# Cross-attention with a routed block: queries and keys in matmuls of 512 columns for four batches, GpSimd's instructions in an alternating order, and another order of the first slots

## The reference

```python
b, tq, _ = input.shape                      # 128, 128, 256
q = (input @ Wq + bq).reshape(b, tq, H, D).transpose(0, 2, 1, 3)
kv = (encoded_features @ Wkv + bkv).reshape(b, tk, 2, H, D).transpose(2, 0, 3, 1, 4)
scores = jnp.einsum('bhqd,bhkd->bhqk', q, kv[0]) / math.sqrt(D)
attn = jax.nn.softmax(scores, axis=2)
out = jnp.einsum('bhqk,bhkd->bhqd', attn, kv[1])
out = out.transpose(0, 2, 1, 3).reshape(b, tq, H * D) @ Wo + bo
...
scores = jnp.einsum('bld,d->bl', x, w_router)           # routed block
_, top_idx = jax.lax.top_k(scores, int(L * 0.75))       # 96 of 128 tokens
processed = jax.nn.gelu(jnp.einsum('bkd,de->bke', selected, w_block))
out = x.at[batch_idx, top_idx].set(processed)
...
x = x + attention(layernorm(x), ctx_1024)
x = x + routed_block(layernorm(x))
```

## Time and profile before

| | us |
|---|---|
| median of 3 runs | 902.03 (901.85 to 904.2) |
| the profiled execution, its device time | 903.28 |
| its span, first to last instruction | 901.5 |
| PE busy in the span | 868.3 (96%) |
| PE weight load | 755.4 (84%) |
| DVE | 854.4 (95%) |
| ACT | 872.5 (97%) |
| POOL | 795.0 (88%) |

### The profile page before, as it was taken

How to read it: one execution, slowest core, us unless ns; L and a number is a source line. 1 busy time by engine, 2 the same in 40 slices (tenths; PEclk the granted TensorE clock), 3 DMA queues, 4 the chain that set the end, 5 groups by cost and what they waited for, 6 DMA issues and landing times. The chain is left out here.

```text
span 901.5 us, 31626 instructions
## 1 busy us (share of the span) xinstructions
PE 868.3 (96%) x10562; PEld 755.4 (84%) x10562; DVE 854.4 (95%) x2068; ACT 872.5 (97%) x4632; POOL 795.0 (88%) x1487
## 2 busy tenths in 40 slices
PE   7899999999999999999999999999999999999972
PEld 6688888888888888888888888888888888888852
DVE  6889999999999999999999999999999999999987
ACT  5899999999999999999999999999999999999984
POOL 4568889999999999999999999999999999998865
PEclk9999999999999999999999999999999999999996
DMA  6221223233233223223223233223222222312102
GB/s 202 61 68 51 65 67 93 59 87 93 59 88 96 59 86 95 59 87 94 69 78 92 60 89 91 76 71 91 79 73 88 82 70 86 96 43 55 49 25 93
DMA packets 70978, 70.48 MB, mean 78 GB/s; under 512 B 12064, under 2 KB 62752, under 8 KB 70816
## 3 DMA queue, kind: packets, MB, share of 16 engines
q1 hardware_dynamic: 69456, 67.68, 26.2%
q10 hardware_dynamic: 1360, 0.79, 0.3%
HBM read 35.13 MB, written 16.78 MB: 58 GB/s over the span
## 5 line engine op out<-in xcount | busy, mean ns | idle before, releaser
L593 ACT ACTIVATE e_sb<-ps_s,neg_max 128x128 f32<-128x128 f32 x2048 | 770.0, 607 | 3.6 <-DVE neg_max L751 3.3
L593 ACT ACTIVATION_READ_ACCUMULATOR e_sb<-ps_s,neg_max 128x1 f32 x2048 | 704.0, 431 | 0.0
L751 DVE TENSOR_REDUCE neg_max<-ps_s 128x4 f32<-128x512 f32 x512 | 331.8, 668 | 25.8 <-PE ps_s L349 24.4
L349 PE MATMUL ps_s<-q_eo,k_sb 32*128 32x256 f32 x2048 | 146.6, 400 | 2.3 <-DVE recip L804 1.4
L414 PE MATMUL ps_a<-e_sb,v_pad 128*32 128x128 f32 x4096 | 138.4, 276 | 2.1 <-POOL v_pad L1085 0.9
L310 PE MATMUL ps_a<-w_o_sb,o_sb 128*128 128x256 f32 x512 | 133.2, 383 | 3.2 <-DVE v_sb L858 3.0
L414 PEld LDWEIGHTS ps_a<-e_sb,v_pad 128*32 128x32 f32 x4096 | 104.1, 109 | 23.7 <-issue 21.3
L349 PEld LDWEIGHTS ps_s<-q_eo,k_sb 32*128 32x128 f32 x2048 | 94.0, 184 | 30.8 <-issue 26.0
L1085 POOL TENSOR_TENSOR v_pad<-v_sb,recip 128x256 f32<-128x256 f32 x128 | 79.7, 623 | 31.8 <-DVE recip L811 29.8
L1074 POOL TENSOR_TENSOR x_sb<-x_sb,bo_sb 128x256 f32<-128x256 f32 x128 | 106.2, 831 | 0.2
L303 PE MATMUL ps_t<-w_z_hi,xt_hi 128*128 128x258 f32 x256 | 96.4, 376 | 2.2 <-DVE z_sb L870 2.2
(11 more groups left out here) (109 smaller groups left out, 2465.5 us busy)
## 6 DMA issues: line engine op xcount, KB each, us to landing
x_sb<-in_x SPq DMA_DIRECT2D x64, 256.0 KB, 2.9
c_sb<-in_ctx SPq DMA_DIRECT2D x64, 256.0 KB, 3.1
out<-z_sb SPq DMA_DIRECT2D x64, 256.0 KB, 2.4
q_eo<-q_raw SPq DMA_DIRECT2D x504, 32.0 KB, 2.0
z_sb<-in_L_xattn_Wkv ACTq DMA_DIRECT2D x2, 256.0 KB, 7.4
z_sb<-in_L_xattn_Wq ACTq DMA_DIRECT2D x1, 256.0 KB, 4.2
w_z_sb<-in_L_ffn_w_block SPq DMA_DIRECT2D x1, 256.0 KB, 7.7
w_o_sb<-in_L_xattn_Wo SPq DMA_DIRECT2D x1, 256.0 KB, 7.0
```

Source lines behind the costliest of these rows:

```text
L349: mm = nc.tensor.matmul(ps_s[:, bank(b, j), c, :, :], k_sb[rows, r2, c, h * T:(h + 1) * T], q_eo[rows, r2, :, c, h, :], start=True, stop=True)
L593: last = nc.scalar.activation(e_sb[:, b % 4, j, c, par, :], ps_s[:, bank(b, j), c, par, :], ACT.Exp, bias=neg_max[:, b % 4, h:h + 1], accu ...
L751: nc.vector.tensor_reduce(neg_max[:, b % 4, :].rearrange("p (c j q) -> p j c q", c=C, j=J)[:, j, :, :], ps_s[:, bank(b, j), :, :, :], AX.X ...
```

## The change

1. *Queries and keys.* From batch 8 on they are made for four batches at once. In step s the new `queries_or_keys(s)` makes one half of the features (m) of queries (s mod 4 = 0, 1) or keys (2, 3) of batches 4(s div 4) + 4 to + 7, in six matmuls of 512 columns. DVE's `queries(b, m)` and `keys(b, m)` add the bias as a column of scalars (tensor_scalar). The first eight batches keep pairs (`..._of_pair`). SP copies each half as it comes, eight DMAs in each of two steps.
2. *Distance and rings.* Inputs are transposed eight batches ahead (LEAD = 8) instead of five; steps 2 and 3 take two batches each. `t_hi` and `t_lo` hold three groups of four batches, `e_sb` three batches, x 18.
3. *POOL's order* in a step: instructions with one tensor and scalars take turns with those of two tensors. The variance and the root of `rstd1` and `rstd2` are parted, with `values_over_sums` between them; `gelu_product` comes a step later.
4. *First slots.* `queries(2)` before `weights_low("v")`; `scores(1)` and its exps before the block weights' mean and the inputs of batch 5; more context loads ahead of the first query DMAs on SP.
5. *The router's keep row* is transposed from 128 rows, the others zero, with three more memsets or parts of memsets at the start of POOL.

```diff
+    RX = 18
+    LEAD = 8
+    FIRST_QUAD = 8
...
-        t_hi = sb("t_hi", [P, 4, 2, C, 2 * T], f32r)
+        t_hi = sb("t_hi", [P, 3, 2, C, 4 * T], f32r)
...
-        e_sb = sb("e_sb", [P, 4, J, C, 2, T])
+        e_sb = sb("e_sb", [P, 3, J, C, 2, T])
...
+            def queries_even_odd(b, m):
+
+                if has(b) and b >= FIRST_QUAD:
+                    n = (b // 4) % 2
+                    sp.wait_ge(q_raw_ready, b + 2 + 2 * m)
+                    if m == 0:
+                        sp.wait_ge(s_mm[J - 1], b - 4)
                     for par in range(2):
                         for j in range(J):
                             rows = slice(32 * j + D * par, 32 * j + D * par + D)
-                            sp.dma_start(q_eo[rows, n, par, :, :, :], q_raw[rows, n, :, :, :]).then_inc(q_eo_in[n], 16)
+                            sp.dma_start(q_eo[rows, n, par, m, :, :], q_raw[rows, m, :]).then_inc(q_eo_in[n], 16)
...
+            for s in range(3, B + 18):
+                if s % 4 == 0:
+                    queries_even_odd(s + 4, 0)
+                elif s % 4 == 1:
+                    queries_even_odd(s + 3, 1)
+                if s >= 4:
+                    load_c(s + 12)
                 store(s - 17)
-                load_x(s + 13)
+                load_x(s + 15)
...
+            def queries_or_keys(s):
+
+                b, kind, m = s // 4 * 4 + 4, s % 4 // 2, s % 2
+                if not has(b):
+                    return
+                w = "qk"[kind]
+                pe.wait_ge(xt_ready, upto(s - 4))
+                if kind == 0 and m == 0:
+                    pe.wait_ge(t_lo_ready, upto(b + 3))
+                mm = three_terms(ps_q[:, :],
+                                 lambda a, c: (w_hi, w_lo)[a][w][:, c, m * P:(m + 1) * P],
+                                 lambda a, c: (t_hi, t_lo)[a][:, (b // 4) % 3, kind, c, :])
                 mm.then_inc((q_mm, k_mm)[kind], 2)
...
             scores(0)
-            queries_or_keys(2, 0)
+            queries_or_keys_of_pair(2, 0)
             transpose_inputs(4)
-            queries_or_keys(2, 1)
+            queries_or_keys_of_pair(2, 1)
+            scores(1)
             mean_of_block_weights()
             transpose_inputs(5)
-            scores(1)
             values(0)
             transpose_inputs(6)
-            queries_or_keys(4, 0)
-            pair_ready(2)
+            queries_or_keys_of_pair(4, 0)
+            transpose_inputs(7)
+            queries_and_keys_ready(2)
             attention(0)
 
             for s in range(2, B - 1):
                 sure = 20 <= s < B - 8
                 scores(s)
-                transpose_inputs(s + 5, s > 2)
+                if s < 4:
+                    transpose_inputs(2 * s + 4)
+                else:
+                    transpose_inputs(s + LEAD, s > 4)
                 values(s - 1)
-                queries_or_keys(s + 2, 1, sure)
-                queries_or_keys(s + 3, 0, sure)
+                if s < 4:
+                    queries_or_keys_of_pair(2 * s, 1)
+                else:
+                    queries_or_keys(s)
                 keep_columns(s - 16)
                 candidates(s - 12)
                 projection(s - 2, sure)
-                pair_ready(s + 1, sure)
-                inputs_ready(s + 6)
+                queries_and_keys_ready(s + 1)
+                if s < 4:
+                    transpose_inputs(2 * s + 5)
+                if s == 2:
+                    queries_or_keys_of_pair(6, 0)
+                if s >= 4:
+                    inputs_ready(s + LEAD + 1)
                 block_product(s - 4, sure)
...
             exps(0, 1)
             exps(0, 0)
+            exps(1, 3)
             inputs_high(5)
-            exps(1, 3)
             exps(1, 2)
             inputs_high(6)
             exps(1, 1)
+            inputs_high(7)
...
-                inputs_high(s + 5, sure)
+                inputs_high(s + LEAD if s >= 4 else 2 * s + 4)
                 exps(s, 3, sure)
                 exps(s, 2)
+                if s < 4:
+                    inputs_high(2 * s + 5)
                 exps(s, 1)
...
+            def queries(b, m):
+
+                if has(b):
+                    dve.wait_ge(q_mm, b + 2 + 2 * m)
+                    if b == FIRST_QUAD:
+                        dve.wait_ge(q_eo_pair_in[4], 128)
+                        dve.wait_ge(q_eo_pair_in[6], 128)
+                    else:
+                        dve.wait_ge(q_eo_in[(b // 4 - 1) % 2], stripes(b - 4))
+                    nc.vector.tensor_scalar(q_raw[:, m, :], ps_q[:, :], bq_sb[:, m:m + 1], None,
                                             ALU.add).then_inc(q_raw_ready, 2)
...
             for j in (3, 2, 1, 0):
                 maxima(0, j)
+            queries_of_pair(2)
             weights_low("v")
-            queries(2)
             inputs_low(4)
+            inverse_sums_23(0)
+            keys_of_pair(2)
             stats1_of_pair(6)
-            keys(2)
-            centre_block_weights()
-            inverse_sums_23(0)
             maxima(1, 3)
             maxima(1, 2)
+            centre_block_weights()
+            inverse_sums_01(0)
+            maxima(1, 1)
             inputs_low(5)
-            inverse_sums_01(0)
             values_and_bias(0)
-            maxima(1, 1)
             maxima(1, 0)
             inputs_low(6)
+            inverse_sums_23(1)
             stats1_of_pair(8)
-            queries(4)
-            inverse_sums_23(1)
+            queries_of_pair(4)
+            inputs_low(7)
+            stats1_of_pair(10)
...
-                normalise(s + 7, sure)
-                rstd1_of_pair(s + 9)
-                rstd2_of_pair(s - 4)
-                gelu_square(s - 5, sure)
+                normalise(s + LEAD + 1, sure)
+                gelu_square(s - 5)
+                variance1_of_pair(s + 11)
+                variance2_of_pair(s - 4)
                 values_over_sums(s - 1, sure)
+                root1_of_pair(s + 11)
+                root2_of_pair(s - 4)
                 scale_and_shift(s - 16)
                 unprocessed(s - 16, sure)
+                input_and_bias(s + 2)
                 gelu_factor(s - 5)
+                gelu_product(s - 8)
                 gelu_sum(s - 7)
-                input_and_bias(s + 4)
                 gelu_cubic(s - 5)
-                gelu_product(s - 7)
```

More of the change, by code:

```diff
@@ L152, in landed, with pair_x, landed_x @@
             return b // R * 16 + 16
-        x_in = [sem(f"x_in{i}") for i in range(8)]
+        def pair_x(b):
+            return b % RX // 2
+        def landed_x(b):
+            return b // RX * 16 + 16
+        x_in = [sem(f"x_in{i}") for i in range(RX // 2)]
         c_in = [sem(f"c_in{i}") for i in range(8)]
@@ L245, in store, with queries_even_odd_of_pair @@
                                  z_sb[:, b % R:b % R + 2, 0:E]).then_inc(stored[pair(b)], 16)
-            def queries_even_odd(b):
-                if b % 2 == 0 and b >= 2 and has(b):
-                    n = (b // 2) % 2
-                    if b == 2:
-                        sp.wait_ge(q_eo_zero, 1)
-                    sp.wait_ge(q_raw_ready, upto(b + 1))
-                    if has(b - 4):
-                        sp.wait_ge(s_mm[J - 1], upto(b - 3))
+            def queries_even_odd_of_pair(b):
+                if b == 2:
+                    sp.wait_ge(q_eo_zero, 1)
+                if b == 4:
+                    sp.wait_ge(q_eo_zero, 2)
+                sp.wait_ge(q_raw_ready, b + 2)
+                n, h = (b // 4) % 2, b % 4
+                for par in range(2):
+                    for j in range(J):
+                        rows = slice(32 * j + D * par, 32 * j + D * par + D)
+                        sp.dma_start(q_eo[rows, n, par, :, h:h + 2, :],
+                                     q_raw[rows, :, h * T:(h + 2) * T]).then_inc(q_eo_pair_in[b], 16)
+            def queries_even_odd(b, m):
[4 more added lines that the diff above has]
+                        sp.wait_ge(s_mm[J - 1], b - 4)
                     for par in range(2):
@@ L386, in transpose_x1 @@
                     pe.wait_ge(x1_ready, upto(b))
-                if b % 2 == 1:
-                    pe.wait_ge(k_ready, upto(b + 5))
-                else:
-                    pe.wait_ge(q_raw_ready, upto(b + 6))
-                if not has(b + 6):
+                slot = b + 3
+                quad = slot // 4 * 4 + 4
+                if has(quad):
+                    pe.wait_ge((q_raw_ready, k_ready)[slot % 4 // 2], quad + 2 + slot % 2 * 2)
+                else:
                     pe.wait_ge(xt_ready, upto(b - 1))
@@ L441, in block_product @@
                     pe.wait_ge(xt_ready, upto(b))
-                pe.wait_ge(t_lo_ready, upto(b + 9))
-                if has(b - 1) and not has(b + 9):
+                pe.wait_ge(t_lo_ready, upto(b + LEAD + 4))
+                if has(b - 1) and not has(b + LEAD + 4):
                     pe.wait_ge(z_ready, upto(b - 1))
```

(19 more changed lines are left out.)

206 lines of the change are left out of this document (110 added, 96 removed).

## The result

| | us |
|---|---|
| before, median of the runs beside it | 901.94 |
| changed kernel, median of 4 runs | 918.07 (917.63 to 920.34) |
| ratio | 1.0181, 95% interval 1.0168 to 1.0193 |
| span of the profiled execution | 916.4 (before 901.5) |

The change makes the kernel 1.8% slower, 16 us by the medians (the two profiled executions differ by 14.9). The range given ended at 906.5.

The account below looks back on a forecast made before the run. ACT was taken as the bound, 0.06 us a step over PE. First slots +0.9 and plateau waits -1.1 gave -0.2 us on 902.03, so 901.8 us; range 897.5 to 906.5.

Parts of the forecast that it names:

- The bound: Plateau: ACT, without holes at 6.69 us a step, bounds the kernel by 0.06 us over PE's 6.63.
- GpSimd: POOL's order in a step: the power delays unprocessed, using most of the 0.37 us before DVE's final; no loss forecast.
- DVE in the router's steps: Slower rival: DVE's additions in five router steps of eight lose 0.34 us in each of 14 rounds; 907.7 us, chance 0.12.
- POOL's alternation: POOL in each step: alternating instruction kinds removes some 3.5 seams, 0.25 us, worth 0 as nobody waits for POOL.
- Evictions: DVE's 512-wide bias addition as tensor_scalar: 0.65 us, +0.05 a step, hidden behind its wait except in router steps.
- Products of 512: PE's query and key matmuls: six of 512 columns for twelve save 0.07 us a step, hidden behind ACT.
- First slots: Start of the kernel: ACT's waits, laid out place by place, sum to 5.0 us against 4.1, 0.9 us lost.

Follow-up runs that it names:

- e7: The kernel before with tanh over only 16 of its 256 columns, so less work for ACT; 901.51 us, ratio 0.9993.
- e6: The changed kernel with DVE's final moved behind the two bn_stats and the evictions as tensor_tensor again; 900.03 us, ratio 0.9977 to the kernel before.
- e12: The changed kernel with POOL's power (root1, root2) moved behind input_and_bias; 912.95 us, ratio 1.0106 to the kernel before.
- e4: The changed kernel with the bias of queries and keys added by the old tensor_tensor; 918.01 us, ratio 1.0175 to the kernel before.

## Why the prediction was wrong

- *The bound.* That ACT has no hole was right, that it is the bound by 0.06 us was wrong: e7 took 1.6 us a round off ACT for 0.09. PE in plain steps and, by the sum under e7, DVE in the router's steps stood level with it. So DVE had little room in the router's steps, and most of its 1.83 us of idle time a round lay in the others.
- *GpSimd.* This is the step that failed. It put the power on the way to `unprocessed`, compared the places on POOL and DVE, and said that it "uses most of that" 0.37 us: the changed kernel's rows show `final` starting 0.05 us after unprocessed's end in the step above, 0.03 to 0.66 over the plateau. But it priced the meeting as a wait for a semaphore, nothing or 0.05. What stands behind `unprocessed` is now a 0.73 us instruction that starts at once, where it was one of 0.41 about to end, and `final` waits for its end. Cost: 0.26 a step, 2.1 us of DVE's work a round. The keep row's 0.29 a round has the same form: in 12 of its 16 instances its record ends 0.08 behind the gelu's square and is 0.53 to 0.55 long.
- *The sum on DVE.* 2.1 for `final`, 8 x 0.06 = 0.5 for the evictions, 0.3 for the keep row: 2.9; measured 54.60 - 51.80 = 2.8. DVE's idle time paid 1.54 of it, and the round grew by the other 1.26.
- *The rival "DVE in the router's steps"* named the engine, and the loss does come out at the end of those steps. Its 0.12 was too small a chance. It lost 0.34 a round, since it added 0.05 and 0.05 a step for 0.06 and 0.26, and in five steps for eight. The range ended at 906.5, short of that rival's own 907.7.
- *POOL's alternation*, of which the prediction said "nobody in the plateau waits for POOL, so this is worth 0": DVE's `final` waits for it without a semaphore, and the list of waits showed nothing of it.
- *Evictions:* 0.65 forecast, 0.66 measured. *Products of 512:* 0.07 forecast, 0.02 to 0.05 measured.
- *First slots.* Most places came as laid out. ACT's timeline of the changed kernel:

```profile
23.95 0.37 ACT L646 ACTIVATE e_sb<-ps_s,neg_max 128x128 f32<-128x128 f32 x1 [0.74 <-DVE neg_max L805]
...
27.39 0.59 ACT L657 CAST t_hi<-ps_t 128x512 fp32r<-128x512 f32 x1 [0.26 <-PE ps_t L414]
...
36.02 0.59 ACT L657 CAST t_hi<-ps_t 128x512 fp32r<-128x512 f32 x1 [0.69 <-PE ps_t L414]
...
44.14 0.59 ACT L657 CAST t_hi<-ps_t 128x512 fp32r<-128x512 f32 x1 [0.87 <-PE ps_t L414]
...
48.05 0.59 ACT L657 CAST t_hi<-ps_t 128x512 fp32r<-128x512 f32 x1
```

The first exp of batch 1 ends at 24.32 (24.33 forecast), t_hi(12) at 48.64 (48.9). t_hi(6), (7), (8), (9) and (11) lose 0.43, 0.33, 0.61, 0.87 and 1.04 by the ends, for 0.43, 0.31, 0.70, 0.95 and 0.98. t_hi(10) loses 0.13 for 0.29, and (12) to (14) lose 0.78 together for 0.47. With 0.86 for that exp the places lose 5.1 together, for the 5.0 forecast. This part was right in mechanism and size, and the 13.8 us arise elsewhere.

What stays open: what e6's 0.23% comes from, what holds the one long step of e12, and whether another order of POOL keeps the alternation and loses nothing; no such order was tried beyond e12.

## What to carry to other kernels

Before moving an instruction of POOL or DVE, lay the two timelines side by side and look at what each DVE instruction with two operands in SBUF will run beside: an end that follows the other engine's end by a constant, whatever the record's length, is an exclusion, and no list of waits shows it. Look also at which of the two starts first: the other one pays, and an order that is free on one engine can hand the bill to another. Two chains that start from the same event and are equally long meet at the same place in every step, and time saved ahead of that place can be spent in it (half of it in e4). A kernel with three engines within 1% of each other has no slack to read from busy shares; take work off one engine and see whether the time follows, before calling it the bound.
